# Expert MLP of a routed layer: the down-projection reads its weights through a register on TensorE instead of from a copied ring

## The reference

```python
h = layernorm(x) * (1 + ca) + sa
x = x + ga * banded_attention(h)                  # 8 batches, 256 tokens, 16 heads, C = 128
h = layernorm(x) * (1 + cb) + sb
routing_weights, selected = top_k(h @ gate, 2)    # 8 experts
routing_weights = softmax(routing_weights)
g = einsum('bsh,ehi->ebsi', h, experts_w1)        # I = 512
u = einsum('bsh,ehi->ebsi', h, experts_w3)
hid = silu(g) * u
eo = einsum('ebsi,eih->ebsh', hid, experts_w2)    # the down-projection
x = x + gb * einsum('ebsh,bse->bsh', eo, tok_w)   # tok_w: the two weights of each token
```

## Time and profile before

| | |
|---|---|
| median of three runs | 401.96 us |
| the profiled execution | 402.63 us |
| its span, first to last instruction | 400.8 us |
| PE busy | 287.4 us (72%) |
| DVE busy | 261.4 us (65%) |
| ACT busy | 166.0 us (41%) |
| the 39 copies at L1020 | 17.4 us of DVE, 447 ns each on the mean |

### The profile page before, as it was taken

How to read it: one execution, slowest core, us unless ns; L and a number is a source line. 1 busy time by engine, 2 the same in 40 slices (tenths; PEclk the granted TensorE clock), 3 DMA queues, 4 the chain that set the end, 5 groups by cost and what they waited for, 6 DMA issues and landing times. The chain is left out here.

```text
span 400.8 us, 7076 instructions
## 1 busy us (share of the span) xinstructions
PE 287.4 (72%) x2281; PEld 208.9 (52%) x2281; DVE 261.4 (65%) x703; ACT 166.0 (41%) x355; POOL 180.8 (45%) x249
## 2 busy tenths in 40 slices
PE   0540859798979898969996324988888888888600
PEld 0310425354545454535544223988888888888600
DVE  8593687777798979876955796444444444445345
ACT  1210226474657465645682012444444444444231
POOL 7850003333454445543574025366555555555321
PEclk9999987899999899998998555999999999999955
DMA  5013131545536462220100001111111111112082
GB/s 158 20 45 107 56 102 41 152 156 124 182 107 217 115 202 94 72 100 5 48 14 16 13 1 29 26 41 40 39 39 39 39 39 39 39 39 39 26 235 79
DMA packets 30488, 29.83 MB, mean 74 GB/s; under 512 B 3080, under 2 KB 24472, under 8 KB 30464
## 3 DMA queue, kind: packets, MB, share of 16 engines
q1 hardware_dynamic: 27648, 24.02, 19.9%
q0 software_dynamic: 2496, 5.12, 4.8%
q10 hardware_dynamic: 320, 0.40, 0.4%
HBM read 21.64 MB, written 7.82 MB: 73 GB/s over the span
## 5 line engine op out<-in xcount | busy, mean ns | idle before, releaser
L771 DVE TENSOR_REDUCE negm<-psA 128x4 f32<-128x1024 f32 x64 | 78.3, 1223 | 33.4 <-PE psA L1140 32.4
L404 ACT ACTIVATE probs<-psB 128x512 f32<-128x512 f32 x128 | 72.1, 596 | 48.3 <-PE psB L1162 47.6
L552 POOL TENSOR_SCALAR_AFFINE_SELECT probs<-probs 128x512 f32<-128x512 f32 x64 | 42.4, 686 | 66.8 <-ACT probs L404 66.8
L1137 PE MATMUL psA<-kd,qs 96*128 96x512 bf16 x128 | 51.0, 420 | 22.3 <-DMA kd<-parts_d 21.8
L1296 PE MATMUL psA<-kd,probs 128*128 128x128 f32 x416 | 53.3, 283 | 15.0 <-DVE kd L1004 15.0
L642 POOL DMA_INDIRECT y_d<-kd,sca_idx x39 | 39.6, 1015 | 45.9 <-ACT kd L463 41.5
L1296 PEld LDWEIGHTS psA<-kd,probs 128*128 128x128 f32 x416 | 50.1, 197 | 17.3 <-DVE kd L1004 17.1
L1162 PE MATMUL psB<-qs,kd 128*128 128x256 bf16 x256 | 48.1, 290 | 2.2 <-DMA qs<-mT 1.4
L1004 DVE COPY kd<-psO 128x128 f32<-128x128 f32 x39 | 11.4, 292 | 57.8 <-remote 33.2
L637 POOL DMA_INDIRECT kd<-h_d,gat_idx x39 | 38.3, 983 | 18.5 <-issue 8.2
L1305 PE MATMUL psM<-probs,kd 128*128 128x128 f32 x312 | 41.3, 275 | 0.4 <-ACT kd L463 0.4
(11 more groups left out here) (188 smaller groups left out, 443.2 us busy)
## 6 DMA issues: line engine op xcount, KB each, us to landing
w_sb<-in_L_ffn_experts_w_dram SPq DMA_DIRECT2D x12, 512.0 KB, 6.6
parts_d<-parts SPq DMA_DIRECT2D x8, 384.0 KB, 3.2
mod_sb<-mod_d SPq DMA_DIRECT2D x8, 320.0 KB, 4.7
probs<-y_d SPq DMA_DIRECT2D x8, 256.0 KB, 4.9
qs<-parts_d SPq DMA_DIRECT2D x16, 96.0 KB
kd<-parts_d SPq DMA_DIRECT2D x16, 96.0 KB
qs<-parts_d SPq DMA_DIRECT2D x16, 64.0 KB
kd<-parts_d SPq DMA_DIRECT2D x16, 64.0 KB
```

What stands on the lines that cost most here:

```text
L404: nc.scalar.activation(probs[:, kt, n % PRING], psB[:, kt, :].rearrange("p (h q) -> p h q", h=H2), ACT.Exp).then_inc(s["exped"], 1)
L552: nc.gpsimd.affine_select(out=u, in_=u, compare_op=ALU.is_ge, fill=0.0, base=0, pattern=[[0, 2 * H2], [-sign, P]], channel_multiplier=sign ...
L771: nc.vector.tensor_reduce(negm[:, b % 2, :, :, j], psA[:, n % 2].rearrange("p q (h k) -> p q h k", h=H2), AX.X, ALU.max, negate=True).then ...
L1137: nc.tensor.matmul(psA[:, n % 2, qt, :].rearrange("p (h k) -> p h k", h=H2), qs[0:SROWS, r, j, qt * P:(qt + 1) * P], kd[0:SROWS, r, :, j, ...
```

## The change

The ring of copies of `w2` and the copies into it are gone. `down(n)` now reads the expert's number into a register of PE, after its two waits, and its four matmuls address `w2_sb` by that register. The lines of PE's code stand 7 or 8 lower in the new file (`up` L1288, `xs_T` L1279, the register load L1296, the matmuls L1298, the loop L1315).

```diff
-        w1_t, w3_t, w2_t = (ybuf[:, i * TRING * I:(i + 1) * TRING * I].rearrange("c (r i) -> c r i", i=I) for i in range(3))
+        w1_t, w3_t = (ybuf[:, i * TRING * I:(i + 1) * TRING * I].rearrange("c (r i) -> c r i", i=I) for i in range(2))
...
-            def w2_copy(n, r, e):
-
-                nc.vector.tensor_copy(w2_t[:, r], w2_sb[:, bass.ds(e, 1)].rearrange("p o k c -> p (o k c)"))
-
...
-            for r in range(2):
-                w2_copy(r, r, expert(r))
...
-                    w2_copy(n + 2, (r + 2) % TRING, e)
...
-            w2_copy(NTILE - 1, 2, e)
...
                 if not first(n):
                     pe.wait_ge(s["y_ready"], n)
+                e = pe.value_load(tile_e[0:1, bass.ds(n, 1)], min_val=0, max_val=E - 1)
                 for k in range(NC):
-                    last = nc.tensor.matmul(psY, hid[:, r, k * P:(k + 1) * P], w2_t[:, r, k * C:(k + 1) * C],
+                    last = nc.tensor.matmul(psY, hid[:, r, k * P:(k + 1) * P], w2_sb[:, bass.ds(e, 1), k].rearrange("p o c -> p (o c)"),
                                             start=(k == 0), stop=(k == NC - 1))
```

## The result

The changed kernel took 403.31 us (median of 20 runs, 401.81 to 405.64), the kernel before 401.47 over 20 runs of the same sessions (398.79 to 404.04). The ratio is 1.0059, with a 95% interval from 1.0039 to 1.0079: slower by 0.6%, where 412.5 us was forecast. The profiled execution took 404.56 us, with a span of 402.8.

A forecast was written before the change was run, and what follows sets the result against it. PE was taken to bound the expert stage, with a pause after each round's branch. 402.63 + 0.7 (last tile) + 9.9 (between rounds) = 413.2; that execution being 0.67 above the median, 412.5 us was forecast, 397 to 416 for 8 in 10.

The forecast's parts named there:

- What bounds the kernel: Expert stage: PE has little room, DVE has room; PE pauses 1.4 us between rounds, 11 times, 15.0 us in all.
- The removal, 0: Taking 39 copies of w2, 17.4 us, off DVE was counted as 0, since DVE already waits for PE.
- The sign given for it: DVE's idle time ahead of L1004 was to grow by about 17 us, and nothing else to move.
- Inside a round, 0: PE's load chain before each down-projection, about 0.7 us, was to stay hidden behind queued array work of 1.28 us.
- the 2.9 that was named as a sign of being wrong: A step inside a round longer than 2.9 us, against 2.79, was to prove the prediction wrong.
- The last tile, +0.7: Nothing lies ahead of the last down-projection, so the whole load chain shows once: +0.7 us, between 0.55 and 1.2.
- From one round to the next, +9.9: PE's loop branch comes later, and DVE's release and PE's restart slide with it: 0.9 us, eleven times.
- 25 had been forecast: PE's idle time ahead of the up-projection was to be 2.3 us instead of 1.4, 11 times.
- No slide: Rival: PE's restart between rounds does not move with the later branch; 402 to 403 us, 30 in 100.
- neither of the two ways: The lag follows the array, or the transpose's word goes out ahead of the later branch.
- my reason against it: Against the rival of an unmoved restart: the 3.0 us from branch to DVE's release repeat to the tenth.

The follow-up runs named there:

- e3: Kernel before with two of the four matmuls of each down-projection left out: 398.81 us, ratio 0.994.
- e6: Changed kernel without the register load, all down-projections reading expert 0's weights in place: 400.73 us, ratio 0.9984.
- e9: Changed kernel with POOL's scatter left out for all but the last three tiles: 384.39 us, ratio 0.9509 to the kernel before.
- e2: Kernel before with POOL's scatter left out for all but the last three tiles: 384.2 us, ratio 0.9597.
- e1: Kernel before with PE's loop over the rounds written out, so no branch on PE: 401.01 us, ratio 0.9999.
- e10: Kernel before with all gathers but the first three left out, scatters kept: 382.37 us in a single run.
- e8: Kernel before, unedited, run once more for a second profile: 400.99 us in a single run, stage 128.6 us.
- e7: Kernel before with PE's register load added, its value unused, copies and matmuls as before: 403.08 us, ratio 1.0025.
- e4: Changed kernel with the register load moved ahead of the down-projection's two waits: 402.66 us, ratio 1.0069 to the kernel before.
- e12: Same kernel as e4, run again on another chip: 407.76 us, ratio 1.0102 to the kernel before.
- e5: Kernel before with the expert stage's indirect DMAs moving 64 rows instead of 128, except first three gathers and last three scatters: 402.61 us, ratio 1.0044.

## Why the prediction was wrong, step by step

- **What bounds the kernel.** The gap between two rounds was read as 1.4 us of a PE-bound stage. It is the mark of another bound: without the second indirect DMA per tile the stage is 113 us, which is PE's own pace, and with it 128 to 134. PE's 8 and 9 tenths are high, but not the limit (e3).
- **The removal, 0.** Right in the time: e6, 0.9984. The sign given for it did not come: DVE's idle time ahead of L1004 grew from 56.8 us to 59.3 (250 to 382 us), not by 17.
- **Inside a round, 0.** Right where nothing else disturbs: steps of 2.79 us in e9. Under the pauses some exposure shows: the changed kernel's PE loader waits 3.0 us in 6 places ahead of a down-projection, 1.4 of them the last tile's, and six steps of its loop are 3.1 to 3.4 us long (the one between the transposes at 300.63 and 303.72, for one), over the 2.9 that was named as a sign of being wrong.
- **The last tile, +0.7.** Right: +0.77; without the pauses 1.19 of idle time in e9 against 0.45 in e2, +0.74.
- **From one round to the next, +9.9.** This step failed. The branch moves by 1.0 us as worked out, but the lag is not bound to it: e1 has the lag and no branch, and the lag goes when a tile has one indirect DMA instead of two (e2, e10). So the 0.9 us a round did not arise, and PE's pauses came to 12.7 us where 25 had been forecast. The 3.0 us from branch to release in the earlier trace rows were a coincidence that repeats, since in that execution every round of the loop brings branch and scatter at the same distance; in e8, the same kernel, it is gone. The trace of the kernel before already held a warning, the first of the eleven pauses, which has no branch ahead of it. The stall at a taken branch, of which the Trainium skill, "Runtime: NRT & Kernel Launch", section "Instruction fetch mechanics", speaks, is not seen in these runs: without the branch (e1) the time is the same, ratio 0.9999.
- **The rivals.** "No slide" (402 to 403, 30 in 100) came about in the time, though by neither of the two ways that I gave it: the lag follows neither the array nor the branch. That the lag repeats to the tenth behind the branch, my reason against it, was no reason: everything in a steady loop repeats to the tenth.

Of the 0.59% that were measured, the last tile's 0.77 us and the 0.17 of the first step (2.96 us for 2.79, as in e9) are 0.23%. Where the rest, 0.9 to 1.4 us, arises is open. It goes with the load in so far as e7, e4 and e12 are slower and e6 is not. But the two profiled executions, 1.9 us apart, differ by only 0.2 us in the stage; the stage begins 1.6 us later with the change (249.04 against 247.48), behind work that the change does not touch. Nor is the longer pattern of pauses with the change a reason: from one late copy to the next it has 13.2 us for four tiles (292.81 to 306.00), which is 3.3 us per tile, and the kernel before 10.0 us for three, which is 3.3 us as well. Two more things stay open: why PE's words, and not POOL itself, are late when indirect DMAs follow each other closely, and what ends the lag. That the DVE copies of w2 have to do with it is excluded by e6, where they are gone and the pauses are not.

None of these that does all the work is faster than the kernel before: e1 is the same, e4, e7 and e12 are slower. e2 and e10 show what would gain, one indirect DMA per tile, but the tile needs both, and each indirect DMA of this kernel takes one column of row indices, one per partition; whether one could serve several tiles was not tried.

## What to carry to other kernels

A wait whose releaser the trace does not know should not be given to the event that stands at a fixed distance ahead of it until all engines' rows around a wait of this kind and around one without it have been set side by side; here POOL's rows told them apart and PE's did not. Every one of the waits should be looked at, the first too, and a second profile of the unchanged kernel is the cheapest experiment of all: e8 would have parted branch and lag before any edit. Before costing an edit on a busy engine, ask what the stage's pace would be without it: here an engine that is busy 8 or 9 tenths was paced by the DMAs of another that is busy for 2.0 of every 3.3 us. A register load ahead of a matmul was hidden where the array had 1.3 us of work queued, and cost its full 0.8 us where it had none.

## What the runs showed of the hardware

- Two indirect DMAs of 128 rows per 2.79 us step did not keep up: 3.2 to 3.4 us per tile (stages of 124.9, in e3, to 134.3 us over 39 tiles in all kernels with both DMAs), although POOL was busy for only 2.0 us of each (0.97 and 0.99), or 2.6 with the 0.30 us of idle time that it shows ahead of each at the least; with one per tile there was no lag. Halving the rows left the lag as it was (e5).
- The lag shows as PE's matmuls recorded on time and their words late by up to 2.0 us, two arriving together: in the kernel with the change, the transpose recorded until 303.99 and the down-projection recorded until 304.89 were acted upon at 306.00 and 306.16.
- A register load on PE takes 0.30 us, with the register instructions around it 0.91 us from y_copy's end to the first matmul, and did not disturb matmuls that were queued (2.79 us steps in e9). The Trainium skill, "DMA: Bandwidth & Descriptors", section "Latency and other measured facts", has some 600 ns as the floor of such a load; the 0.30 us here disagree.
